# The carried state of a chunked linear attention, multiplied in 32x32 TensorE tiles for all sequences at once

## The reference

```python
q = feature_map(LN(x) @ Wq.T + bq);  k = feature_map(LN(x) @ Wk.T + bk)   # elu + 1
v = LN(x) @ Wv.T + bv
kv_cum = cumsum(einsum('bhtd,bhte->bhtde', k, v), axis=2)
numerator = einsum('bhtd,bhtde->bhte', q, kv_cum)
denominator = maximum(einsum('bhtd,bhtd->bht', q, cumsum(k, axis=2)), 1e-6)
x = x + LN((numerator / denominator) @ Wo.T + bo)
xd = mx_quantise(LN(x))           # blocks of 32, 6-bit grid, then scaled back
x = x + LN(xd @ wd.T + bias)      # wd: the weights, quantised the same way
```

## Time and profile before

| | |
|---|---|
| median of 3 runs | 2627.73 us (2625.16 to 2629.82) |
| the profiled execution | 2631.21 us, of which the traced span is 2629.4 us |
| PE busy / PEld busy | 2518.0 us (96%) / 2062.7 us (78%) |
| DVE busy | 2148.7 us (82%) |
| ACT busy / POOL busy | 1143.0 us (43%) / 1055.4 us (40%) |
| mean granted TensorE clock | 0.992 of 2.4 GHz |

### The profile page before, as it was taken

How to read it: one execution, slowest core, us unless ns; L and a number is a source line. 1 busy time by engine, 2 the same in 40 slices (tenths; PEclk the granted TensorE clock), 3 DMA queues, 4 the chain that set the end, 5 groups by cost and what they waited for, 6 DMA issues and landing times.

```text
span 2629.4 us, 62366 instructions
## 1 busy us (share of the span) xinstructions
PE 2518.0 (96%) x24082; PEld 2062.7 (78%) x24082; DVE 2148.7 (82%) x4177; ACT 1143.0 (43%) x2058; POOL 1055.4 (40%) x1482
## 2 busy tenths in 40 slices
PE   5999999999999999999999999999999999999996
PEld 4778778778778778778787787787787877877885
DVE  6788888888888888888888888888888888888885
ACT  4444444444444444444444444444444444444442
POOL 1234444344443334443334433344433444434443
PEclk8999999999999999999999999999999999999998
DMA  4011101111011111011111011110111110011110
GB/s 151 20 43 48 42 30 32 40 48 44 30 38 40 40 48 44 28 34 38 48 48 35 30 39 40 48 44 28 40 38 42 48 41 31 32 40 48 32 33 17
DMA packets 57483, 107.55 MB, mean 41 GB/s; under 512 B 6768, under 2 KB 7152, under 8 KB 56816
## 3 DMA queue, kind: packets, MB, share of 16 engines
q1 hardware_dynamic: 57456, 107.18, 12.7%
HBM read 73.60 MB, written 33.55 MB: 41 GB/s over the span
## 4 chain that ended last, share of the span: by engine, by line
PE 45%; DVE 37%; issue 11%; ACT 4%; POOL 2%; DVEq 1%; ACTq 0%; POOLq 0%; DMA 0%; SPq 0%
PE work L343 10%; PE work L345 8%; PE work L344 8%; DVE kc L830 6%; PE score L434 4%; PE work L360 4%; PE work L460 4%; DVE QT L811 3%; PE work L453 3%; DVE A L873 3%; DVE KT L811 3%; DVE bn_x L788 2%; DVE amax L898 2%; DVE bn_r L788 2%; DVE bn_f L788 2%
## 5 line engine op out<-in xcount | busy, mean ns | idle before, releaser
L873 DVE TENSOR_TENSOR A<-score,causal 128x512 f32<-128x512 f32 x512 | 317.5, 683 | 42.7 <-PE score L434 42.7
L597 ACT ACTIVATE o_buf<-x_res,shift_r,rs_r 128x512 f32<-128x512 f32 x128 | 104.3, 815 | 395.6 <-POOL shift_r L1048 395.6
L1055 POOL TENSOR_TENSOR x_res<-x_res,o_buf 128x512 f32<-128x512 f32 x128 | 179.4, 1402 | 209.5 <-ACT o_buf L597 209.5
L593 ACT CAST xT_hi<-work 128x512 fp32r<-128x512 f32 x128 | 74.6, 583 | 396.5 <-PE work L360 396.5
L343 PE MATMUL work<-wv_hi,xT_hi 128*128 128x512 f32 x512 | 216.9, 424 | 0.0
L343 PE MATMUL score<-xT_hi,wk_hi 128*128 128x512 f32 x512 | 208.4, 407 | 6.3 <-issue 6.3
L343 PE MATMUL work<-wo_hi,oT_hi 128*128 128x512 f32 x512 | 206.2, 403 | 2.9 <-DVE oT_lo L880 2.6
L1045 POOL TENSOR_TENSOR rs_f<-ve_f,minus_half 128x1 f32<-128x1 f32 x128 | 70.1, 548 | 342.6 <-DVE ve_f L792 342.6
L343 PE MATMUL score<-xT_hi,wq_hi 128*128 128x512 f32 x512 | 205.1, 401 | 0.0
L345 PE MATMUL work<-wo_hi,oT_lo 128*128 128x512 f32 x512 | 203.3, 397 | 0.0
L344 PE MATMUL work<-wo_lo,oT_hi 128*128 128x512 f32 x512 | 203.1, 397 | 0.0
(11 more groups left out here) (130 smaller groups left out, 6750.6 us busy)
## 6 DMA issues: line engine op xcount, KB each, us to landing
x_in<-in_x SPq DMA_DIRECT2D x128, 256.0 KB, 2.9
x_res<-in_x SPq DMA_DIRECT2D x128, 256.0 KB, 2.6
out<-f_buf SPq DMA_DIRECT2D x96, 256.0 KB, 2.0
out<-xd SPq DMA_DIRECT2D x32, 256.0 KB, 2.0
V<-in_wk SPq DMA_DIRECT2D x1, 1024.0 KB, 7.1
QT<-in_wq SPq DMA_DIRECT2D x1, 1024.0 KB, 7.9
kc<-in_wo SPq DMA_DIRECT2D x1, 1024.0 KB, 9.7
A<-in_wf SPq DMA_DIRECT2D x1, 1024.0 KB, 11.5
```

What stands on the lines that cost most here:

```text
L873: nc.vector.tensor_tensor(A[:, j, :, :], score_bank[j][:], causal[:].unsqueeze(1).to_broadcast([P, G, P]), ALU.mult).then_inc(a_set, 1)
L1055: nc.gpsimd.tensor_tensor(x_res[:, b, :], x_res[:, b, :], o_buf[:, b % 2, :], ALU.add).then_inc(r_set, 1)
```

## The change

**The product with the state.** The four L453 matmuls of each `attend(b)` go. In their place `past_products()` runs once in a turn, ahead of all scores: 64 matmuls for the four sequences, each with a 32x32 block of `S` as weights (`S` is now 128 x 4 x 4 x 32, without zeros) and 128 columns of Q, head j of group g reading partitions 32j and writing partitions 32g of `score_bank[j]`. ACT copies the four banks to SBUF (`past(j)`, buffer `past_att`), and for each sequence copies its part back into the PSUM bank that `attend(b)` is going to use (`seed(b)`). The V x A matmuls then add to it. The rows of the attention result come out in another order of heads, and `Wo` is permuted on the host to match.

**The state copy.** `S` is filled by one ACT copy of 128x512 at the end of the turn, in place of 16 copies of 32x128.

**Queues and banks.** `v(0)` stands ahead of `denominators`, `f(3)` ahead of `spread`; `v(1)`, `v(2)` and `v(3)` stand around `past_products` and `scores(0)`, and no longer between the sequences. Bank order, ACT, DVE and POOL queues are rewritten to go with it. `o_bias(b)` waits in addition for `q8_set` of b-2, `kn(b)` on ACT for `st_mm`. A 256-byte spacer and two moved bias buffers change SBUF addresses; `past_att` is new.

The diff, cut to its core:

```diff
-    (("f", 2), W2), (("xd", 3), W1), (("den", 0), W0), (("v", 0), W2), (("kn", 0), W1), (("f", 3), W0),
...
+    (("f", 2), W2), (("xd", 3), W1), (("v", 0), W0), (("den", 0), W2), (("kn", 0), W1), (("f", 3), W0),
+    (("v", 1), W1), (("v", 2), W2), (("v", 3), W0), (("x", 0), W1), (("att", 0), W2),
...
-        S = sb("S", [P, NSEQ, G, P])
+        S = sb("S", [P, NSEQ, G, DH])
+        past_att = sb("past_att", [P, NSEQ, HPG, P])
...
+        sb("spacer", [P, 64])
...
                 def scores(b):
                     if cur:
                         if b == 0:
-                            pe.wait_ge(qn_set, count(i, 3))
+                            pe.wait_ge(past_set, count(i, HPG - 1))
...
-                def attend(b):
-                    if cur:
-                        take(i, ("att", b), here, before)
+                def past_products():
+                    if cur:
                         if first:
                             pe.wait_ge(state_zeroed, 1)
                         else:
-                            pe.wait_ge(s_set, count(i - 1, b))
-                        att = by_group(bank(("att", b))[:])
-                        for g in range(G):
-                            nc.tensor.matmul(att[:, g, :], S[:, b, g, :], QT[:, g, b * P:(b + 1) * P],
-                                             start=(g == 0), stop=False, skip_group_check=True)
+                            pe.wait_ge(s_set, count(i - 1, 0, 1))
+                        wait_apart(pe, qn_set, count(i, 3))
+                        for b in range(NSEQ):
+                            for g in range(G):
+                                for j in range(HPG):
+                                    rows = slice(j * DH, (j + 1) * DH)
+                                    last = nc.tensor.matmul(score_bank[j][g * DH:(g + 1) * DH, b, :], S[rows, b, g, :],
+                                                            QT[rows, g, b * P:(b + 1) * P], start=True, stop=True)
+                        last.then_inc(past_mm, 1)
+
+                def attend(b):
+                    if cur:
                         pe.wait_ge(a_set, count(i, b * HPG + HPG - 1, 16))
                         pe.wait_ge(v_set, count(i, b))
+                        pe.wait_ge(seeded, count(i, b))
...
+                v(0)
                 denominators()
-                v(0)
                 kn(0)
+                f(3)
                 spread()
-                f(3)
+                v(1)
+                past_products()
+                v(2)
                 scores(0)
-                v(1)
+                v(3)
                 x_transposes(0)
                 attend(0)
...
-                def state(b):
-                    if cur:
-                        act.wait_ge(st_mm, count(i, b))
-                        for j in range(HPG):
-                            rows = slice(j * DH, (j + 1) * DH)
-                            last = nc.scalar.copy(S[rows, b, :, rows], state_bank[rows, b, :, :])
-                        last.then_inc(s_set, 1)
+                def past(j):
+                    if cur:
+                        act.wait_ge(past_mm, count(i, 0, 1))
+                        nc.scalar.copy(past_att[:, :, j, :], score_bank[j][:]).then_inc(past_set, 1)
+
+                def seed(b):
+                    if cur:
+                        take(act, i, ("att", b), {0}, set())
+                        if b == 0:
+                            act.wait_ge(past_set, count(i, HPG - 1))
+                        nc.scalar.copy(bank(("att", b))[:],
+                                       past_att[:, b, :, :].rearrange("p j t -> p (j t)")).then_inc(seeded, 1)
+
+                def state():
+                    if cur:
+                        act.wait_ge(st_mm, count(i, NSEQ - 1))
+                        nc.scalar.copy(S[:], state_bank[:]).then_inc(s_set, 1)
```

157 lines of the change are left out of this document (85 added, 72 removed).

## The result

The changed kernel takes **2804.97 us** (median of 4 runs, 2804.19 to 2805.98) against 2628.78 us of the kernel before in the same session: a ratio of 1.0673, 95% interval 1.0657 to 1.0689. The prediction was 2537 us, faster, with a range of 2488 to 2605. It was wrong by 268 us and in sign. The profiled execution took 2805.98 us, its span is 2804.2 us, the mean granted clock 0.962.

The account below looks back on a forecast made before the run. PE's own work was taken as the bound, DVE second. Gains of 130 + 55 us less 67 for added passes and shape changes and 28 for a new wait made 90 us: 2627.7 to 2537 us, range 2488 to 2605.

Parts of the forecast that it names:

- The sum as a whole: Whole kernel: 130 + 55 gained, 67 and 28 lost, 90 us faster, giving 2537 us.
- Removed L453: PE's four fp32 matmul groups with the state go: 4.06 us a turn, 130 us in 32 turns.
- removed waits: PE's waits on DVE ahead of sequence 3's L453 and the denominators go: 28.4 and 26.9 us, together 55.
- added group: 64 small matmuls on PE, 128 passes at 14.9 ns: 1.9 us a turn, bounds 1.1 and 4.7.
- shapes: Extra changes of tile shape on PE around the new group and scores: 0.2 us a turn.
- The chain ahead of the scores: DVE's multiplications and ACT's copies around past_products, just covered by v(1) and v(2): counted 0.
- between the sequences: PE's 6.3 us between V x A products against DVE's 5.7 to 6.8 us: nearly even, counted 0.
- ACT: ACT's busy time goes from 35.3 to 36.5 us a turn, nothing on the path.
- Queue order on DVE, a new wait: DVE's 39.7 to 40.3 us against 38.9 of PE work: 0.9 us wait a turn, at most 1.5.
- The collisions of DVE and POOL: Four q8 operations lose 1.8 us a turn to POOL; reordered queues may avoid collisions or make more.
- The rival "slower": Small matmuls on PE don't overlap at all: 15.4 us a turn more, 3030 us; slower had chance 0.07.
- a turn above 78.5 us: Sign at the loop's turn, forecast at 77.1 us: above 78.5 would prove the sum wrong.

Follow-up runs that it names:

- the last version: Changed kernel plus small matmuls before the loop, DVE and ACT exchanges, next tile's statistics (sequence 0 too) moved, q(3)'s exponential ahead of f_norm(1): 2526.24 us, ratio 0.961.
- the base: Changed kernel with 31 small matmuls once in front of the loop, nothing in the loop changed: 2665.93 us, ratio 1.014.
- the two exchanges: Against 2665.9 us: on DVE xd_lo(2) ahead of f_bias(1) and its statistics, on ACT q(2)'s exponential ahead of f_norm(1): 2606.53 us, ratio 0.9914.

## Why the prediction was wrong, by its steps

**The sum as a whole.** The last version has all of the changed kernel's work, no stall at the jumps back and no wait at the denominators. With it the result splits: 2628.8 - 2526.2 = 102 us gained, 2665.9 - 2526.2 = 140 us lost to waits behind the queues of DVE and ACT, and 139 us to the fetch: 2629 - 102 + 140 + 139 = 2806. The prediction had 130 + 55 - 67 = 118 for the first, 28 for the second, and no line for the third. The first term isn't the change's alone: the last version also makes statistics elsewhere that the kernel before made in the same stretch. Whether that kernel would gain by the same moves wasn't run; its two waits on DVE, 28.4 and 26.9 us, are within the 118.

**Removed L453, removed waits, added group, shapes.** Right. The group costs what was taken (61.0 us, 14.9 ns a pass), L453 and the two old waits are gone, and PE is busy for 75.80 us a turn in the last version, where about 76 was forecast. The reason given for 14.9 ns, that the issue of instructions is the limit, was tested by no run, so the price is right and its reason open. That the turn takes 76.90 where 77.1 was forecast is in part luck, since this version has moves that the prediction knew nothing of.

**The chain ahead of the scores, between the sequences.** Right, though each was called even with nothing to spare: no wait ahead of the scores, the new group or the V x A products stands among PE's waits, in the changed kernel or in the last version.

**ACT.** Its total was right, 35.7 us in the turn from 1218.39 where 36.5 was taken. "Nothing on the path" was wrong: the place of one exponential in ACT's queue is worth 128 us (2734.4 against 2606.5).

**Queue order on DVE, a new wait: the step that failed, in size and in method.** It took the DVE work of the stretch as one length (39.7 to 40.3 us against 38.9 of cover) and set the wait at 0.9 us, 1.5 at most. Measured without the fetch: 96.1 + 34.5 + 9.0 us, nearly all inside the loop, and PE busy 41 us longer than in the last version (2484.8 against 2443.9), at a mean granted clock of 0.978 against 0.994. The step asked when DVE would be done with everything and looked at the last customer, the denominators, with the 2.9 us of `v(0)` as new cover. But `f(2)` is a customer in the middle, and `v(0)` stands behind it. There the cover stayed what it was, 1258.85 - 1226.27 = 32.6 us; the kernel before had `xd_lo(2)` ready at 1257.97, 0.9 us early; and the step's own 3.0 us of new work come ahead of it. That alone makes 2.1 us a turn where 0.9 was taken, from rows of the kernel before. In the base DVE came 4.6 us later (31.0 to 35.6), and `f(1)` and `f(2)` together wait 0.91 + 2.92 us; the 1.6 us beyond the 3.0 were not split by any run, but DVE stands still there for 2.3 us, in three waits for ACT and POOL, against 1.3 in two before. In the queue `xd_lo(2)` also stood behind `f_bias(1)` and its statistics, with 1.84 us that it didn't need. Nor did the step look at ACT and POOL, whose totals are under half of a turn: `f_norm(1)` stood still for 8.2 us in ACT's queue with exponentials behind it. By the last runs the 140 us are 59 for the two exchanges, 44 for the statistics moved out of the stretch, and 36 for the statistics of sequence 0 together with the exponential of `q(3)`.

**The collisions of DVE and POOL.** Left open whether the reordering would avoid them; it moved them. The mean of `q8` went down, from 1132 ns to

```profile
L944 DVE TENSOR_TENSOR q<-o_buf,rxs 128x512 fp8e4<-128x512 f32 x128 | 107.0, 836 | 23.0 <-DVE rxs L942 8.9
L1083 POOL TENSOR_TENSOR rs_f<-ve_f,minus_half 128x1 f32<-128x1 f32 x128 | 97.2, 759 | 250.9 <-DVE ve_f L828 250.9
```

in the base, 4 x 0.3 = 1.2 us a turn less, and the scans, the small copies behind them (0.17 or 1.09 us, mean 390 ns before and 613 in the base) and POOL's pow (0.55 or 1.43 us) got longer. That these are the same kind of collision is read from the durations alone. DVE's busy time didn't fall (2157.6 us against 2148.7). "A `q8` mean under 0.8 would show the collisions gone" was a bad test for that reason: it looked at one victim.

**What the prediction had no step for: the fetch.** The diff adds more passes to the loop than it takes away; the count of instructions rises from 1547 to 1732, and the page's row of the instruction queue, with 18 packets for a kernel of 32 turns, could have raised the question of how far that is from the limit. The rival "slower" had picked the price of the small tiles, a term that turned out exact. The test that was named, a turn above 78.5 us, did show the sum wrong.

## What to carry to other kernels

Count the instructions of a hardware loop's body, and look at the instruction queue's packets in the profile: a wait on nothing ("issue") of several microseconds at the first instruction of each turn, together with packets in proportion to the turns, was a fetch here (0.2 us of it stand there in the kernels without one too), and before any work is taken out of the loop, some 110 to 125 cheap instructions in front of it (28 to 31 small matmuls here) may remove it. For a stretch with two full engines, a sum of lengths up to its end is not enough: make it for each operation that the full engine waits for, with only the cover that stands ahead of that operation. Walk each queue of each engine to every operation that the full engine waits for, and ask what stands ahead of it that it doesn't need, also on engines that are mostly idle. Where two queues hold the same wait, a repair in one of them can cost time until the other is repaired as well, so try them together.

## What the runs showed of the hardware that was not expected

- A loop body of 1732 instructions on PE cost 3.4 to 4.0 us at each jump back and some nine packets of 16 KB, at one place; 112 to 124 instructions more in front of the loop removed it (2805 to 2666 us), and 80 made it worse (2931 us). At two places only some jumps back stalled, 6 and 24 of 29, each with nine packets.
- A stop of PE of 3.4 to 4.0 us in the changed kernel was followed by matmuls at 1.2 GHz (0.43 us apart instead of 0.23) in every turn, so that it cost 1.4 to 1.7 us more than it lasted in 22 of 29 cases and 2.8 to 2.9 in 7. The wait of 2.9 us ahead of `f(2)` was followed by such matmuls in 17 of 30 turns of the changed kernel and in 22 of 30 of the base, and by none in the others. What makes that difference was not settled.
- Tiles of 32x32 with 128 moving columns passed at 14.9 ns each, sixteen in turn, no faster than 32-column tiles with 32 moving columns.
- Taking 1.1 us of work off DVE, the fullest engine beside PE, made the kernel 12 us slower (2562.0 to 2574.3 us): a chain through ACT's and POOL's queues set the pace, and POOL's `shift_f` in it took 0.68 us in place of 0.27.
